# Image 0's values copied whole and split on GpSimd, with three other steps of the start moved

## Chip, cores and metric

The kernel runs on one core of a Trainium2 chip. The metric is the device time of one execution in microseconds, as the median of several. The profile is one more execution with the hardware profiler on. The engines are TensorE (PE; PEld is its weight load), VectorE (DVE), ScalarE (ACT), GpSimd (POOL) and SyncE (SP), which issues most transfers.

## What is computed

Two layers over x of shape 4 x 128 x 32 x 32 (four images, C = 128 channels, 1024 pixels), float32:

```python
# layer 0, without softmax: g, theta, phi are 1x1 convolutions to 64 channels
pairwise_weight = jnp.matmul(theta_x, phi_x) / N
y = jnp.matmul(pairwise_weight, g_x)
out = x_flat + _conv1x1(y, out_w, out_b)
# layer 1, on layer 0's output x (g = x)
scores = jnp.einsum('ncp,ncq->npq', theta, phi) / jnp.sqrt(c)
attn = jax.nn.softmax(scores, axis=-1)
f = jnp.einsum('npq,ncq->ncp', attn, g)
return x + conv1x1(f, conv1_w, conv1_b)
```

## The kernel before

Layer 0 has no softmax, so for each image it folds into one affine map of x: Z = (I + A) x + d, where A comes from the inner product of phi and g over all pixels. Per image the chain is pg0, pg1 (phi and g of the two halves of x), MT (their inner product), R, A, then Z0, Z1 (two halves of 512 pixels). Layer 1 takes Z: t = U Z + u are the queries with theta and phi folded together, V holds the values with the last convolution folded in, and rho is a row term (one more column of the value product) which goes into the exponent's shift.

Each image has 8 tiles of 128 query rows, 32 tiles in all, numbered n. For a tile: scores(n) (six matmuls of 512 columns into the PSUM `ring`, slot n % 2); row_max(n) on DVE; row_shift(n) on POOL, 128 x 1, from the row maximum and rho; exps(n) on ACT, which also sums the rows; norm(n) on DVE, a reciprocal and a multiplication of P in place; turn(n), eight transposes into the PSUM `turned`; high_turned and low_turned (ACT, DVE), which split the result; and attend, which after every four tiles multiplies values with the turned probabilities into the PSUM bank `numer`. Scores of n + 2 are issued ahead of the turning of n.

Products of float32 precision are made from rounded parts (type fp32r): a value X is split into X_hi, a rounded copy, and X_lo = X - X_hi, and `three` multiplies hi by hi, lo by hi and hi by lo. The rounding is a copy (ACT, or POOL as CAST), the low part a subtraction (DVE or POOL). POOL works on SBUF only here.

All small products of an image pass one after the other through one PSUM bank, `aux`, in the order of `AUX_ORDER`: each is issued on PE when its predecessor has left the bank (`aux_free`). Every engine's program is one list written out by hand, in which `early_job(b, t)` and `late_job(b, t)` place image b's steps in the tiles of image b - 1. An instruction waits for those ahead of it on its engine.

Around the change: image 0's values come in three parts of 3, 3 and 2 chunks of 128 pixels (`V_PARTS`). Parts 0 and 1 go through `numer`, which is free until the first attend, part 2 through `aux` at tile 1. For each, DVE makes the row term (L649), ACT makes V_hi (L506) and DVE V_lo (L654). On PE the start is: phi and g of image 1, t part 0 (one tile), scores(0), value part 0 (L281), t part 1 (three tiles, `turned`), aux job t1 (the rest of t), scores(1), then the loop over n. POOL joins Z from its parts for image 0 (L799), rounds x of image 1 (`high_x` L818, `low_x` L822) in tiles 0 and 1, and splits Z of image 1 (`split_z`, L828 and L830) in tiles 3 and 4. Other lines: L234 inner product, L222 to L224 the three matmuls of `three`, L317 turn, L336 attend, L521 exps, L529 and L682 split of the turned tile, L557 and L712 t of image 0, L643 t_lo, L638 AT_lo, L667 row maximum, L673 and L675 norm, L811 shift. SP's `load(3)` (L193 on) waits for both low parts of image 1's x, whose buffer it overwrites.

## Time and profile before

| | us |
|---|---|
| median of 3 runs | 175.65 (175.43 to 176.45) |
| the profiled execution | 174.63 |
| its span, first to last instruction | 172.8 |
| PE busy in it | 161.3 |
| granted TensorE clock | 1.00 throughout |

The profile's page gives busy time by engine, a strip of 40 slices (4.32 us each) and the costliest groups of instructions. The trace behind it is read by views: busy time by stage, who waited for whom, the timeline. In a timeline row the first number is the start, the second the duration; brackets hold the idle time of the engine just before and what ended it. Durations of queued instructions overlap a little, so distances between starts are the safer measure of pace.

### The profile page before, as it was taken

Reading aid. Unit: us, or ns where it says so; the run is one execution under the profiler, and the core shown is the slowest. Engines: PE = TensorE matmul, PEld = TensorE weight load, DVE = VectorE, ACT = ScalarE, POOL = GpSimd, SP = SyncE. Lnnn points to the kernel's source line nnn. Section 1 sums busy time; section 2 is a strip of 40 time slices with the busy share of each in tenths; the row PEclk is TensorE's granted clock in tenths of the full one; section 3 lists DMA queues with packets and bytes.
Section 4 is the critical chain, followed back from the end, with each engine's and each line's share of the span. In section 5 each row is a group of like instructions: output and inputs, shape, how many; then the busy total and the mean of one; then the engine's idle time right before and its main releaser. Section 6 shows DMA issues by size and latency. Waiting matters only on the chain.

```text
span 172.8 us, 2602 instructions
## 1 busy us (share of the span) xinstructions
PE 161.3 (93%) x967; PEld 134.2 (78%) x967; DVE 126.2 (73%) x217; ACT 95.1 (55%) x178; POOL 64.9 (38%) x73
## 2 busy tenths in 40 slices
PE   7789893986999999999999999999999999998994
PEld 6667682765888898787888898787898888886893
DVE  1316698779698897567898887567899889899512
ACT  3024554576765572567766573567766566667410
POOL 1006016526622257226624256216625252834020
PEclk9999999999999999999999999999999999999999
DMA  4703000020000001000000101000000101000111
GB/s 138 197 0 121 4 0 0 14 109 0 4 2 0 0 4 61 0 0 0 4 0 0 61 4 63 0 0 0 4 0 4 61 0 65 0 0 0 61 61 64
DMA packets 2829, 4.76 MB, mean 28 GB/s; under 512 B 448, under 2 KB 1280, under 8 KB 2816
## 3 DMA queue, kind: packets, MB, share of 16 engines
q1 hardware_dynamic: 2304, 4.39, 7.2%
q10 hardware_dynamic: 512, 0.20, 0.7%
q8 instruction: 8, 0.13, 0.3%
q14 instruction: 5, 0.04, 0.1%
HBM read 2.49 MB, written 2.10 MB: 27 GB/s over the span
## 4 chain that ended last, share of the span: by engine, by line
PE 83%; DVE 8%; DMA 3%; POOL 2%; ACT 2%; issue 1%; SPq 0%; ACTq 0%
PE numer L336 22%; PE turned L317 15%; PE ring L222 8%; PE ring L224 8%; PE ring L223 8%; DVE negmax L667 3%; PE aux L281 3%; DMA X<-x_dram 3%; PE aux L228 3%; PE aux L343 2%; PE aux L234 2%; PE aux L222 2%; PE aux L223 1%; PE aux L224 1%; DVE P L675 1%; PE ring L383 1%
## 5 line engine op out<-in xcount | busy, mean ns | idle before, releaser
L811 POOL TENSOR_SCALAR shift<-negmax,rho 128x1 f32<-128x1 f32 x32 | 27.9, 871 | 82.7 <-DVE negmax L667 78.1
L667 DVE TENSOR_REDUCE negmax<-ring 128x1 f32<-128x1024 f32 x32 | 39.1, 1223 | 18.5 <-PE ring L224 18.1
L521 ACT ACTIVATE P<-ring,shift 128x1024 f32<-128x1024 f32 x32 | 35.8, 1119 | 9.8 <-POOL shift L811 9.6
L682 DVE TENSOR_TENSOR PT_lo<-turned,PT_hi 128x512 fp32r<-128x512 f32 x62 | 39.8, 681 | 0.9 <-ACT PT_hi L529 0.9
L529 ACT ACTIVATE PT_hi<-turned 128x512 fp32r<-128x512 f32 x62 | 33.7, 596 | 9.3 <-PE turned L317 9.3
L317 PE MATMUL turned<-identity,P 128*128 128x128 f32 x256 | 33.6, 274 | 0.6 <-DVE PT_lo L682 0.6
L317 PEld LDWEIGHTS turned<-identity,P 128*128 128x128 f32 x256 | 29.5, 141 | 4.0 <-DVE P L675 1.0
L222 PE MATMUL ring<-Z_hi,t_hi 128*128 128x512 f32 x64 | 26.5, 414 | 0.6 <-DVE t_lo L712 0.6
L224 PE MATMUL ring<-Z_lo,t_hi 128*128 128x512 f32 x64 | 25.2, 394 | 0.0
L223 PE MATMUL ring<-Z_hi,t_lo 128*128 128x512 f32 x64 | 25.1, 393 | 0.0
L675 DVE TENSOR_SCALAR P<-P,rden 128x1024 f32<-128x1024 f32 x32 | 24.1, 754 | 1.1
L336 PE MATMUL numer<-PT_hi,V_hi 128*128 128x512 f32 x56 | 24.4, 435 | 0.0
L336 PE MATMUL numer<-PT_lo,V_hi 128*128 128x512 f32 x56 | 22.1, 395 | 0.0
L336 PE MATMUL numer<-PT_hi,V_lo 128*128 128x512 f32 x56 | 22.1, 394 | 0.0
L222 PEld LDWEIGHTS ring<-Z_hi,t_hi 128*128 128x128 f32 x64 | 12.0, 188 | 3.9 <-DVE t_lo L712 1.2
L224 PEld LDWEIGHTS ring<-Z_lo,t_hi 128*128 128x128 f32 x64 | 12.0, 188 | 2.8
L223 PEld LDWEIGHTS ring<-Z_hi,t_lo 128*128 128x128 f32 x64 | 12.1, 188 | 2.2
L336 PEld LDWEIGHTS numer<-PT_hi,V_lo 128*128 128x128 f32 x56 | 10.5, 187 | 2.5
L336 PEld LDWEIGHTS numer<-PT_lo,V_hi 128*128 128x128 f32 x56 | 10.6, 190 | 1.3
L336 PEld LDWEIGHTS numer<-PT_hi,V_hi 128*128 128x128 f32 x56 | 10.6, 189 | 1.3
L838 POOL TENSOR_TENSOR result<-attended,Z 128x512 f32<-128x512 f32 x7 | 9.0, 1287 | 4.2 <-ACT attended L539 4.2
L501 ACT ACTIVATE t_hi<-aux,U 128x512 fp32r<-128x512 f32 x7 | 4.8, 689 | 9.1 <-PE aux L224 9.1
(116 smaller groups left out, 198.0 us busy)
## 6 DMA issues: line engine op xcount, KB each, us to landing
out_dram<-result SPq DMA_DIRECT2D x7, 256.0 KB, 2.0
X<-x_dram SPq DMA_DIRECT2D x3, 512.0 KB, 3.3
X<-x_dram SPq DMA_DIRECT2D x2, 256.0 KB, 4.4
out_dram<-result SPq DMA_DIRECT2D x1, 192.0 KB, 1.9
w<-weights_dram SPq DMA_DIRECT2D x1, 128.0 KB, 5.8
wi<-inner_dram ACTq DMA_DIRECT2D x1, 64.2 KB, 5.6
pg_w<-pg_weights_dram ACTq DMA_DIRECT2D x1, 64.0 KB, 3.6
pg_b<-pg_bias_dram ACTq DMA_DIRECT2D x1, 64.0 KB, 5.6
```

The costliest lines, as they stand in the source:

```text
L222: nc.tensor.matmul(to, left_hi, right_hi[:, cols], start=first, stop=False)
L223: nc.tensor.matmul(to, left_lo, right_hi[:, cols], start=False, stop=False)
L224: return nc.tensor.matmul(to, left_hi, right_lo[:, cols], start=False, stop=last)
L317: mm = nc.tensor.transpose(turned[:, j * TILE:(j + 1) * TILE], P[:, n % P_BUFFERS, j * TILE:(j + 1) * TILE], identity[:, :])
L336: mm = nc.tensor.matmul(numer[:, :], left[:, b % 2, chunk], right[:, g, j, :], start=(j == 0 and n == 0), stop=(j == TILES - 1 and n == 2))
L521: nc.scalar.activation(P[:, n % P_BUFFERS, :], ring[:, n % 2, :], ACT.Exp, bias=shift[:, t:t + 1], accum_out=den[:, t:t + 1]).then_inc(pro ...
L529: nc.scalar.activation(PT_hi[:, group % GROUPS, half_chunks(half), k * TILE:(k + 1) * TILE], turned[:, columns(half)].rearrange("p (j r) - ...
L667: nc.vector.tensor_reduce(negmax[:, t:t + 1], ring[:, n % 2, :], AX.X, ALU.max, negate=True).then_inc(max_ready, 1)
L675: nc.vector.tensor_scalar(P[:, n % P_BUFFERS, :], P[:, n % P_BUFFERS, :], rden[:, t:t + 1], None, ALU.mult).then_inc(probs_normed, 1)
L682: nc.vector.tensor_tensor(PT_lo[:, group % GROUPS, half_chunks(half), rows], turned[:, columns(half)].rearrange("p (j r) -> p j r", j=CHUN ...
L811: nc.gpsimd.tensor_scalar(shift[:, t:t + 1], negmax[:, t:t + 1], rho[:, b % 2, t:t + 1], rho[:, b % 2, t:t + 1], ALU.subtract, ALU.add).th ...
L838: nc.gpsimd.tensor_tensor(result[:, g, :], attended[:, g, :], Z[:, b % Z_BUFFERS, columns(g)], ALU.add).then_inc(result_ready, 1)
```

## The change

Image 0's value part 2 leaves `aux` for `numer`, as the other two. ACT now makes the row term of each part and one plain copy of the part into V_plain (the buffer that was V_last), in place of V_hi; the copy frees `numer`. POOL makes V_hi and V_lo of image 0 from V_plain, part by part, behind row_shift(0), (2) and (4). DVE makes neither for image 0. On PE, t part 1 is issued ahead of value part 0, the aux job t1 behind scores(1), value part 1 still behind turn(0) and value part 2 behind turn(1); on DVE t1's low part comes behind row_max(2). On POOL x of image 1 is rounded ahead of the joins of Z and its low parts are made before and after row_shift(0); Z of image 1 is split in tiles 2 and 3. attend(0, 0) waits for three low parts of V. The other images are treated as before.

```diff
@@ -52,10 +52,10 @@
 JOBS = ("pg0", "pg1", "MT", "R", "A", "Z0", "Z1", "t0", "V0", "V1", "V2", "t1")
-AUX_ORDER = ([(0, "MT"), (0, "R"), (0, "A"), (1, "pg0"), (0, "t1"), (0, "V2")] + [(1, job) for job in JOBS[2:]]
+AUX_ORDER = ([(0, "MT"), (0, "R"), (0, "A"), (1, "pg0"), (0, "t1")] + [(1, job) for job in JOBS[2:]]
              + [(b, job) for b in range(2, IMAGES) for job in JOBS])
 
-SPLIT_ORDER = [(b, job) for b, job in AUX_ORDER if job in ("t0", "V0", "V1", "V2", "t1") or (job == "A" and b)]
+SPLIT_ORDER = [(b, job) for b, job in AUX_ORDER if job in ("t0", "t1") or (b and job in ("A", "V0", "V1", "V2"))]
 
@@ -114,7 +114,7 @@
         PT_lo = sb("PT_lo", [C, GROUPS, TILES, BANK], F32R)
-        V_last = sb("V_last", [C, PIX])
+        V_plain = sb("V_plain", [C, PIX])
         PT_last = sb("PT_last", [C, TILES, TILE])
@@ -144,7 +144,8 @@
         first_t, first_t_hi, first_t_lo = sem("first_t"), sem("first_t_hi"), sem("first_t_lo")
-        first_v, first_v_hi, first_v_lo = sem("first_v"), sem("first_v_hi"), sem("first_v_lo")
+        first_v, first_v_copied = sem("first_v"), sem("first_v_copied")
+        first_v_hi, first_v_lo = sem("first_v_hi"), sem("first_v_lo")
         first_rho = sem("first_rho")
@@ -323,8 +324,9 @@
                         if b == 0:
-                            pe.wait_ge(first_v_lo, 2)
-                        pe.wait_ge(aux_free, aux_after(b, "V2"))
+                            pe.wait_ge(first_v_lo, len(V_PARTS))
+                        else:
+                            pe.wait_ge(aux_free, aux_after(b, "V2"))
                     if group >= 1:
@@ -389,19 +391,19 @@
             scores(0)
+            queries(0, first_t_bank(1), FIRST_T[1]).then_inc(first_t, 1)
             pe.wait_ge(first_z_ready, 1)
...
             value_chunks(0, numer, 0).then_inc(first_v, 1)
-            queries(0, first_t_bank(1), FIRST_T[1]).then_inc(first_t, 1)
+            scores(1)
             job_t(0, 1)
-            scores(1)
-
-            def first_value_part():
-                pe.wait_ge(first_z_ready, 2)
-                pe.wait_ge(first_v_lo, 1)
-                value_chunks(0, numer, 1).then_inc(first_v, 1)
+
+            def first_value_part(part):
+                pe.wait_ge(first_z_ready, HALVES)
+                pe.wait_ge(first_v_copied, part)
+                value_chunks(0, numer, part).then_inc(first_v, 1)
 
@@ -420,8 +422,8 @@
             def late_job(b, t):
-                if t == 0 and b == 1:
-                    job_V(0, 2)
+                if t == 1 and b == 1:
+                    first_value_part(2)
                 if t == 0 and b > 1:
@@ -442,7 +444,7 @@
                 if n == 0:
-                    first_value_part()
+                    first_value_part(1)
                 if n >= GT:
@@ -462,7 +464,7 @@
                 for j in half_range(half):
-                    mm = nc.tensor.matmul(last_tile, V_last[:, j * C:(j + 1) * C], PT_last[:, j, :],
+                    mm = nc.tensor.matmul(last_tile, V_plain[:, j * C:(j + 1) * C], PT_last[:, j, :],
                                           start=(j == 0), stop=(j == TILES - 1))
@@ -557,15 +559,26 @@
 
-            def first_v_high(part):
-                act.wait_ge(first_rho, part + 1)
-                high_values(0, numer, part, first_v_hi)
+            def first_row_terms(part):
+                act.wait_ge(first_v, part + 1)
+                first, last = V_PARTS[part]
+                nc.scalar.activation(rho[:, 0, first:last].rearrange("p (j c) -> p j c", c=1),
+                                     chunks_of(numer, part)[:, :, C:C + 1], ACT.Identity,
+                                     bias=r0).then_inc(first_rho, 1)
+
+            def first_values(part):
+                if part:
+                    first_row_terms(part)
+                first, last = V_PARTS[part]
+                nc.scalar.activation(V_plain[:, first * C:last * C].rearrange("p (j c) -> p j c", c=C),
+                                     chunks_of(numer, part)[:, :, 0:C], ACT.Copy).then_inc(first_v_copied, 1)
 
...
             first_t_high(1)
+            first_row_terms(0)
             exps(0)
-            first_v_high(0)
+            first_values(0)
             high_t(0, 1)
@@ -584,10 +597,10 @@
             def late_job(b, t):
-                if t == 0 and b == 1:
-                    high_V(0, 2)
                 if t == 1:
                     copy_R(b)
+                if t == 1 and b == 1:
+                    first_values(2)
                 if t == 2:
@@ -606,7 +619,7 @@
                 if n == 0:
-                    first_v_high(1)
+                    first_values(1)
                 if n + 2 < ALL:
@@ -713,14 +726,6 @@
 
-            def first_v_low(part):
-                dve.wait_ge(first_v_hi, part + 1)
-                low_values(0, numer, part, first_v_lo)
-
-            def first_row_terms(part):
-                dve.wait_ge(first_v, part + 1)
-                row_terms(0, numer, part).then_inc(first_rho, 1)
-
             first_z_low(0)
@@ -729,13 +734,9 @@
             row_max(0)
-            dve.wait_ge(u_copied, 1)
-            first_row_terms(0)
             first_t_low(1)
...
             row_max(1)
-            first_v_low(0)
-            low_t(0, 1)
 
@@ -750,8 +751,6 @@
             def late_job(b, t):
-                if t == 0 and b == 1:
-                    low_V(0, 2)
                 if t == 0 and b > 1:
@@ -765,15 +764,13 @@
                     row_max(n + 2)
+                if n == 0:
+                    low_t(0, 1)
                 norm(n + 1)
...
                 low_turned(n, 0)
-                if n == 0:
-                    first_row_terms(1)
                 low_turned(n, 1)
-                if n == 0:
-                    first_v_low(1)
             dve.wait_ge(turned_ready, ALL * HALVES)
@@ -784,6 +781,17 @@
         def _(pool):
+            def high_x(b):
+                pool.wait_ge(x_loaded[b], 16)
+                if b >= 2:
+                    pool.wait_ge(aux_free, aux_after(b - 1, "Z1"))
+                nc.gpsimd.tensor_copy(X_hi[:, :], X[:, b % 2, :]).then_inc(x_hi, 1)
+
+            def low_x(b, half):
+                pool.wait_ge(x_hi, b)
+                nc.gpsimd.tensor_tensor(X_lo[:, columns(half)], X[:, b % 2, columns(half)],
+                                        X_hi[:, columns(half)].bitcast(F32), ALU.subtract).then_inc(x_lo, 1)
+
             nc.gpsimd.memset(identity[:, :], 0.0).then_inc(identity_ready, 1)
@@ -794,33 +802,24 @@
             nc.gpsimd.tensor_tensor(UT_lo[:, :], U[:, 0:C], UT_hi[:, :].bitcast(F32), ALU.subtract).then_inc(u_lo, 1)
+            high_x(1)
             for half in range(HALVES):
...
                                         Z_lo[:, 0, columns(half)].bitcast(F32), ALU.add).then_inc(first_z_ready, 1)
+            low_x(1, 0)
 
...
                 if t in (0, 3, 6):
-                    if b == 0 and t < 6:
+                    if b == 0:
                         pool.wait_ge(first_rho, t // 3 + 1)
...
                                         rho[:, b % 2, t:t + 1], ALU.subtract, ALU.add).then_inc(shift_ready, 1)
-
-            def high_x(b):
-                pool.wait_ge(x_loaded[b], 16)
-                if b >= 2:
-                    pool.wait_ge(aux_free, aux_after(b - 1, "Z1"))
-                nc.gpsimd.tensor_copy(X_hi[:, :], X[:, b % 2, :]).then_inc(x_hi, 1)
-
-            def low_x(b, half):
-                pool.wait_ge(x_hi, b)
-                nc.gpsimd.tensor_tensor(X_lo[:, columns(half)], X[:, b % 2, columns(half)],
-                                        X_hi[:, columns(half)].bitcast(F32), ALU.subtract).then_inc(x_lo, 1)
 
@@ -838,7 +837,18 @@
 
+            def split_first_values(part):
+                first, last = V_PARTS[part]
+                cols = slice(first * C, last * C)
+                pool.wait_ge(first_v_copied, part + 1)
+                nc.gpsimd.tensor_copy(V_hi[:, 0, cols], V_plain[:, cols]).then_inc(first_v_hi, 1)
+                pool.wait_ge(first_v_hi, part + 1)
+                nc.gpsimd.tensor_tensor(V_lo[:, 0, cols], V_plain[:, cols], V_hi[:, 0, cols].bitcast(F32),
+                                        ALU.subtract).then_inc(first_v_lo, 1)
+
             row_shift(0)
+            low_x(1, 1)
+            split_first_values(0)
             row_shift(1)
@@ -847,18 +857,20 @@
                 if i + 1 < IMAGES:
-                    if t == 0:
+                    if t == 0 and i:
                         high_x(i + 1)
                         low_x(i + 1, 0)
-                    if t == 1:
+                    if t == 1 and i:
                         low_x(i + 1, 1)
-                    if t == 3:
+                    if n in (0, 2):
+                        split_first_values(1 if n == 0 else 2)
+                    if t == (3 if i else 2):
                         split_z(i + 1, 0)
-                    if t == 4:
+                    if t == (4 if i else 3):
                         split_z(i + 1, 1)
...
                     pool.wait_ge(aux_free, aux_after(i, "t1"))
-                    nc.gpsimd.tensor_tensor(V_last[:, :], V_hi[:, i % 2, :].bitcast(F32),
+                    nc.gpsimd.tensor_tensor(V_plain[:, :], V_hi[:, i % 2, :].bitcast(F32),
                                             V_lo[:, i % 2, :].bitcast(F32), ALU.add).then_inc(v_joined, 1)
```

## Rows read from the trace of the kernel before

**Rows 1.** The page: span, busy time by engine, PE's tenths in 40 slices.

```profile
span 172.8 us, 2602 instructions
...
PE 161.3 (93%) x967; PEld 134.2 (78%) x967; DVE 126.2 (73%) x217; ACT 95.1 (55%) x178; POOL 64.9 (38%) x73
...
PE   7789893986999999999999999999999999998994
```

**Rows 2.** Busy time by stage: length, busy us of PE, PEld, DVE, ACT, POOL.

```profile
60.00:80.00 20.00, 20.00 (x127) 16.81 (x126) 15.10 (x26) 12.01 (x23) 9.06 (x10) 1.00 0.04 14
```

**Rows 3.** Who waited for whom, 14 to 50 us: total us, times, longest.

```profile
PE aux L234 <- DVE V_lo L654: 2.9, 1, 2.9
...
PE aux L222 <- POOL Z_lo L830: 1.4, 1, 1.4
...
PE aux L222 <- DVE AT_lo L638: 0.7, 1, 0.7
```

**Rows 4.** Timeline, first values and t: start, duration, instruction [idle before].

```profile
17.72 0.83 PE L281 MATMUL numer<-VW,Z 128*128 128x130 f32 x6
...
18.31 0.42 PE L222 MATMUL turned<-Z_hi,UT_hi 128*128 128x384 f32 x1
...
19.12 0.58 ACT L557 ACTIVATE t_hi<-turned,U 128x384 fp32r<-128x384 f32 x1 [3.32 <-PE turned L224]
19.38 0.37 POOL L811 TENSOR_SCALAR shift<-negmax,rho 128x1 f32<-128x1 f32 x1 [2.12 <-DVE rho L649]
...
19.73 0.62 DVE L712 SCALAR_TENSOR_TENSOR t_lo<-turned,U,t_hi 128x384 fp32r<-128x384 f32 x1 [0.46 <-ACT t_hi L557]
...
20.41 0.50 PE L222 MATMUL ring<-Z_hi,t_hi 128*128 128x512 f32 x1 [0.64 <-DVE t_lo L712]
```

**Rows 5.** Timeline, 27 to 30 us, ACT, DVE and PE around the long wait.

```profile
27.20 0.49 ACT L506 ACTIVATE V_hi<-numer 128x384 fp32r<-128x384 f32 x1 [1.19 <-DVE rho L649]
27.58 1.11 ACT L521 ACTIVATE P<-ring,shift 128x1024 f32<-128x1024 f32 x1
...
29.23 0.41 DVE L654 TENSOR_TENSOR V_lo<-aux,V_hi 128x256 fp32r<-128x256 f32 x1
...
29.70 1.15 PE L234 MATMUL aux<-pgT 128*64 128x64 f32 x16 [2.89 <-DVE V_lo L654]
```

**Rows 6.** Timeline, 21 to 31 us: norm(0), turn(0), scores(3), a shift.

```profile
21.23 0.75 DVE L675 TENSOR_SCALAR P<-P,rden 128x1024 f32<-128x1024 f32 x1
...
23.27 1.04 PE L317 MATMUL turned<-identity,P 128*128 128x128 f32 x8
...
25.18 0.48 PE L222 MATMUL ring<-Z_hi,t_hi 128*128 128x512 f32 x1
...
30.95 0.92 POOL L811 TENSOR_SCALAR shift<-negmax,rho 128x1 f32<-128x1 f32 x1 [2.02 <-DVE negmax L667]
```

**Rows 7.** Timeline, then groups by shape (busy us, mean ns | idle before).

```profile
27.66 1.27 POOL L822 TENSOR_TENSOR X_lo<-X,X_hi 128x512 fp32r<-128x512 f32 x1
27.72 0.56 DVE L654 TENSOR_TENSOR V_lo<-numer,V_hi 128x384 fp32r<-128x384 f32 x1
...
L799 POOL TENSOR_TENSOR Z<-Z_hi,Z_lo 128x512 f32<-128x512 f32 x2 | 2.5, 1282 | 1.3 <-DVE Z_lo L705 1.3
...
L828 POOL CAST Z_hi<-Z 128x512 fp32r<-128x512 f32 x2 | 1.2, 609 | 0.0
```

**Rows 8.** Timeline, 30 to 46 us: turn(1), row maxima, image 1's t, values.

```profile
30.77 1.09 PE L317 MATMUL turned<-identity,P 128*128 128x128 f32 x8
...
33.85 1.23 DVE L667 TENSOR_REDUCE negmax<-ring 128x1 f32<-128x1024 f32 x1 [0.47 <-PE ring L224]
...
41.83 1.21 DVE L667 TENSOR_REDUCE negmax<-ring 128x1 f32<-128x1024 f32 x1
...
42.93 0.47 PE L222 MATMUL aux<-Z_hi,UT_hi 128*128 128x512 f32 x1 [1.37 <-POOL Z_lo L830]
...
45.97 0.83 PE L281 MATMUL aux<-VW,Z 128*128 128x130 f32 x6
```

## Prediction

> **What bounds the kernel now.** I read four views, from coarse to fine. The page first: TensorE (PE) is busy for 93% of a span of 172.8 us, no other engine comes near [rows 1]. So only time in which PE stands still can be won, unless PE work goes away, and this change takes none away: it has the same matmuls in another order. Its PE line in 40 slices of 4.32 us falls to 3 tenths at 25.9 to 30.2 us and to 6 tenths at 38.9 to 43.2, and is at 9 from there to the tail [rows 1]. Then the busy time by stage: from 60 to 80 us PE is busy for 20.00 of 20.00 us [rows 2]. The room lies in the start, before 46 us, and in the tail, which the diff leaves alone. Third, who waited for whom from 14 to 50 us: PE stood for 2.9 us before the inner product of image 1 (L234) until DVE's V_lo, 1.4 us before t of image 1 until POOL's Z_lo and 0.7 us before Z of image 1 until DVE's AT_lo [rows 3]. The fourth is 0.64 us before scores(1) until t_lo [rows 4]. Together 5.6 us, the most that any reordering of the start could give. Last, the timeline around each wait, for what the releaser itself waited for.
>
> The 2.9 us wait is a long queue. Image 0's values come in three parts. Part 2 sits in the aux bank, which the inner product needs next. Its V_hi on ACT is queued behind exps(2) at 27.58, which is queued behind V_hi of part 1 at 27.20. That one waited 1.19 us for a row term on DVE; V_lo of part 2 ends at 29.64 and PE starts at 29.70 [rows 5].
>
> **The change, part by part.** Times below are of the profiled execution.
>
> *Start.* PE now does the second part of t ahead of value part 0. Value part 0 took from 17.72 to 18.31, when t started; so t starts 0.6 earlier, t_hi ends at 19.1 instead of 19.70, and t_lo follows the row maximum on DVE, at about 19.1 instead of 19.73 [rows 4]. scores(1), before at 20.41, starts at 19.8. But the aux job t1, half of scores(1)'s work, used to lie in the wait ahead of scores(1) and now comes behind it. scores(1) and (2) took 2.86 us together (20.41 to 23.27), so t1 is 0.7, and 19.8 + 2.86 + 0.7 puts turn(0) at 23.35, against 23.27 before [rows 4, 6]. So the start gives nothing to PE; the move costs 0.1.
>
> *The first row term on ACT.* Value part 0 now ends at about 19.15, and ACT makes the term (0.2 us) once t_hi is through. No row has an ACT operation on so few PSUM columns; the bounds are nothing and the 0.49 of V_hi's 384 columns [rows 5]; I take 0.2, nearer the low end, since three columns leave little but the fixed part. Shift(0) then starts at 19.5 instead of 19.38 [rows 4]: exps(0) and norm(0) 0.1 late.
>
> *V_hi, V_lo and row terms leave DVE, a copy takes V_hi's place on ACT.* The ACT copy has V_hi's shape and costs the same 0.49 [rows 5]: nothing. DVE loses three subtractions (0.56, 0.56 and 0.41 us) and three row terms [rows 5, 7]. It is not the bound there, and row_max(2), which stood behind two low parts, starts at 23.6, as soon as scores(2) is ready.
>
> *The split on POOL.* No row has it at 384 columns. The cast took 609 ns for 512 and the subtraction 1.27 us for 512 [rows 7]. Scaled by columns they are 0.46 and 0.96, unscaled 0.61 and 1.27; I take 0.5 and 1.0, near the scaled ends. Part 0's split stands ahead of shift(1) on POOL, and behind it wait exps(1), norm(1) and scores(3). The copy ends at 21.5 on ACT; at that time norm(0) is running on DVE, from 21.3 to 22.1. A shift that meets a norm takes 0.92 where one alone takes 0.37, ending about 0.15 after the norm [rows 4, 6]. So I let the cast begin when the norm is over: 22.1 to 22.6, V_lo to 23.65, shift(1) 23.7 to 24.1 (row_max(1) is done at 23.25). Then exps(1), 1.1 plus the 0.1 until its sums are read, to 25.3, and scores(3) at 25.4 instead of 25.18, PE waiting some 0.4 us for it. With an unhindered cast shift(1) could start at 23.25, which gives 0.3 to 0.4 back; with both unscaled prices it is 0.4 later.
>
> The Trainium skill (SBUF — State Buffer, section "SBUF: two separate sides") says that a DVE operation in a two-port mode and a GpSimd operation hold the shared port pair exclusively, whichever starts first, for the whole instruction. On its first half the trace agrees (0.92 beside a norm, 0.37 alone); that a norm waits behind a POOL operation no row here shows. The same notes (GPSIMD Engine Reference, "Engine selection") advise VectorE for elementwise work, GpSimd being about 2 times slower with two inputs, which speaks against this change; the trace agrees in size, 1.27 us for 512 columns on POOL beside 0.56 for 384 on DVE [rows 7]. By it each subtraction costs some 0.4 us more than on DVE; only part 0's is on the path, and it is in the 0.4 above.
>
> *The wait of 2.9 us.* Part 2 leaves the aux bank, so the inner product waits only for t1's low part. That is placed behind row_max(2): 24.75 to 25.5, before PE gets there. scores(3) from 25.4, the inner product from 26.9 and, with the 1.07 it took from 29.70 to 30.77, turn(1) at 27.95: 2.8 early [rows 5, 8]. Is turn(1) ready? norm(1) ends at 26.4; the low parts of turn(0) end at 27.0 and 27.6. Yes, with 0.3 to spare, and this slack is what covers DVE. Value part 2 now stands behind turn(1): 0.36 us, work that was ahead of scores(3) before. So scores(4) starts 2.5 early, and row_max(4) at 31.35 instead of 33.85 [rows 8]. On POOL, part 1 is split from 27.0 to 28.6 and shift(3) is wanted at 28.9: hidden, by 0.3.
>
> *Rounding of x earlier.* high_x(1) fills POOL's idle 1.3 us before the joins of Z (two half casts of 609 are 1.2) [rows 7]; low_x fills 17.3 to 18.5 and 19.9 to 21.2. Nobody waits. SyncE's load(3), queued behind load(2), waits for both low parts and is released some 12 us earlier; its next store is far off and the queues are empty then. Nothing.
>
> *Z's split one step earlier.* POOL: shift(4) to 33.6 beside norm(3), part 2's split (256 columns, about 1.15) to 34.8, then Z half 0, which ACT makes at 35.5 (before, 2.5 later). Cast and subtraction, 0.6 and 1.3, end at 37.5. PE reaches t of image 1 at 38.9. So the wait of 1.4 us at 42.93 goes, and t starts 4.0 early [rows 3, 8]. The AT_lo wait of 0.7 stays: its chain (scores(4), row maximum, norm, AT_lo) is only shifted. Shift(5) is now behind this split; row_max(5) ends at 37.35, so it is at most 0.1 to 0.2 late, with norm(4) beside it.
>
> *What is late next.* Value part 0 of image 1 needs aux free from t's low part, which DVE makes after row_max(6) and norm(5). Row_max(6) was at 41.83 and moves by 2.5 only, to 39.3, norm(5) ends at 41.4, t_lo at 42.1. PE is there at 41.7: 0.4 of waiting. Value part 0 starts at 42.2 instead of 45.97 [rows 8], and behind it all goes as before, PE full until the tail.
>
> **The sum.** 2.9 + 1.4 less 0.1 (start), 0.1 (scores(3), net of the value part moved behind it) and 0.4 (new wait) is 3.7. The profiled execution had 174.63 us around its 172.8 us span; less 3.7 it is 170.9. The median of three runs is 1.0 higher, 175.65, and from it I predict 171.9.
>
> **Rivals.** (a) *The lock tie, 172.3.* Z_lo of half 0 ends at 37.5, norm(4) wants to start at 37.45. If a norm waits behind a POOL operation and the queued shift slips in first, norm(4) is 0.4 late, and with it row_max(6) and value part 0: gain 3.3. By the skill's rule it would be so; the times are too near to tell. (b) *Unhindered cast, 171.5*: gain 4.1, as above. (c) *Slow splits, 172.7*: unscaled prices in part 0, and part 1's split then in front of shift(3); 0.4 each, gain 2.9. (d) *Half, 173.2*: the 1.4 us is replaced by another wait of the same size (Z half 0 late on ACT behind exps(4), or shift(5) behind the split): gain 2.4. For it: exps(4) and the split are tight in the chain; against it: 1.4 us of room at 38.9. (e) *Nothing, 175.6*: the new ACT and POOL steps set the pace of all early tiles, each exps about 0.6 late over six tiles. Against it: POOL was idle most of this stretch. (f) *Slower, 177*: DVE and POOL exclude each other for all that POOL now does from 19.9 to 37.5, about 7.3 us (1.3 + 1.5 + 1.5 + 1.15 + 1.9), also where DVE runs subtractions, and each exclusion lands on the path. It turns to a loss once more than 3.7 of the 7.3 do; 5 would give 177. Against it: the DVE subtraction at 27.72 took 0.56 for 384 columns with POOL at work beside it (1.5 ns a column), the one at 29.23 took 0.41 for 256 with POOL idle (1.6 a column) [rows 5, 7].
>
> **How the numbers follow.** Forecast 0.44, (a) 0.16, (b) 0.10, (c) 0.11, (d) 0.11, (e) 0.05, (f) 0.03. The range from 171.0 to 173.4 takes in (b) and (d), with 0.5 at the low end for the spread of the runs. About 0.5%, 0.9 us, is what a measurement of this kernel can tell from no change: faster by more 0.92, within 0.05, slower 0.03.
>
> **What would show it.** Of the changed kernel the waits view should have no wait of PE L234 on V_lo, none of t on Z_lo, AT_lo's 0.7 still there, a new wait of about 0.4 before scores(3), released by exps(1), and one of about 0.4 before value part 0 of image 1, released by t_lo. turn(1) should start near 27.95, t of image 1 near 38.9, the value part near 42.2. The POOL cast of part 0 should be lengthened or delayed by norm(0), and the one of part 1 not. Wrong would be the prediction if POOL's split takes over 2 us a part, if the ACT row term costs over half a microsecond, or if PE has new gaps after 46 us.

## The result, and the profile after

| | before | after |
|---|---|---|
| median, us | 176.05 (175.43 to 176.75, 4 executions) | 170.51 (170.28 to 170.84, 4 executions) |
| the profiled execution | 174.63 | 170.84 |
| its span | 172.8 | 169.0 |

The ratio is 0.9686, with a 95% interval of 0.9639 to 0.9733. The forecast was 171.9, and the measured time lies below its range, which began at 171.0. The 176.05 is the median of the three executions known before and a fourth. The two traces differ by 3.8 us, where the sum gave 3.7; the medians differ by 5.5. So there are two questions: whether the 3.8 us went where the prediction said, and where the other 1.7 us come from.

The page of the changed kernel, span, engines and the PE and clock lines of the 40 slices (of 4.2 us each):

```profile
span 169.0 us, 2605 instructions
...
PE 161.8 (96%) x967; PEld 135.2 (80%) x967; DVE 124.1 (73%) x211; ACT 95.8 (57%) x181; POOL 69.1 (41%) x79
...
PE   7889899799999999999999999999999999998994
...
PEclk9999999999999999999999999999999999999999
```

The 3 and the 6 of [rows 1] are gone; PE's busy time is nearly what it was (161.8 and 161.3 us), and the span is 3.8 us shorter.

Who waited for whom from 14 to 50 us, rows of PE, of its weight load and POOL's for the copy on ACT (total us, times, longest):

```profile
POOL V_hi L844 <- ACT V_plain L573: 1.9, 2, 1.5
...
PE aux L223 <- DVE AT_lo L651: 0.9, 1, 0.9
...
PE ring L223 <- DVE t_lo L725: 0.7, 1, 0.7
...
PEld aux L282 <- DVE t_lo L656: 0.5, 1, 0.5
```

The 2.9 and the 1.4 of [rows 3] are not there. AT_lo's wait is still there, 0.9 where 0.7 was, and so is t_lo's before scores(1).

The timeline of the changed kernel, the steps that the prediction put a time to (start, duration):

```profile
19.70 0.50 PE L223 MATMUL ring<-Z_hi,t_hi 128*128 128x512 f32 x1 [0.66 <-DVE t_lo L725]
...
21.29 0.75 DVE L688 TENSOR_SCALAR P<-P,rden 128x1024 f32<-128x1024 f32 x1
...
21.50 0.90 POOL L844 CAST V_hi<-V_plain 128x384 fp32r<-128x384 f32 x1 [0.42 <-ACT V_plain L573]
...
22.48 1.01 POOL L846 TENSOR_TENSOR V_lo<-V_plain,V_hi 128x384 fp32r<-128x384 f32 x1
...
23.27 1.03 PE L318 MATMUL turned<-identity,P 128*128 128x128 f32 x8
...
23.49 0.36 POOL L821 TENSOR_SCALAR shift<-negmax,rho 128x1 f32<-128x1 f32 x1
...
25.23 0.47 PE L223 MATMUL ring<-Z_hi,t_hi 128*128 128x512 f32 x1 [0.25 <-ACT P L523]
...
26.66 0.50 POOL L844 CAST V_hi<-V_plain 128x384 fp32r<-128x384 f32 x1 [1.50 <-ACT V_plain L573]
...
26.79 1.15 PE L235 MATMUL aux<-pgT 128*64 128x64 f32 x16
...
27.86 1.09 PE L318 MATMUL turned<-identity,P 128*128 128x128 f32 x8
...
31.39 1.22 DVE L680 TENSOR_REDUCE negmax<-ring 128x1 f32<-128x1024 f32 x1 [0.80 <-PE ring L225]
...
33.79 0.50 PE L223 MATMUL aux<-X_hi,AT_hi 128*128 128x512 f32 x1 [0.95 <-DVE AT_lo L651]
```

and further on:

```profile
38.94 0.39 PE L223 MATMUL aux<-Z_hi,UT_hi 128*128 128x512 f32 x1
...
42.16 0.94 PE L282 MATMUL aux<-VW,Z 128*128 128x130 f32 x6
```

| step | before | predicted | measured |
|---|---|---|---|
| scores(1) | 20.41 | 19.8 | 19.70 |
| turn(0) | 23.27 | 23.35 | 23.27 |
| shift(1) | 23.43 | 23.7 | 23.49 |
| scores(3) | 25.18 | 25.4 | 25.23 |
| turn(1) | 30.77 | 27.95 | 27.86 |
| row_max(4) | 33.85 | 31.35 | 31.39 |
| t of image 1 | 42.93 | 38.9 | 38.94 |
| value part 0 of image 1 | 45.97 | 42.2 | 42.16 |

Every step is within about 0.2 us. The reader should see three things in the rows. The inner product (L235) starts at 26.79, behind scores(3) and nothing else. The cast of value part 0 took 0.90 us, because it began 0.2 us into norm(0), and the same cast at 26.66, with no norm beside it, took 0.50. And value part 0 of image 1 is held by t_lo, the new last comer: its weight load waits 0.5 us, PE itself loses less (t to value part took 3.04 us before and takes 3.22).

So the first question, where the 3.8 us went, is answered by the traces. The experiments are mostly about the second, and about which part of the change carries which part of the 3.8 us.

### The profile page after: what moved, and what is told of

It is laid out like the page before. It is cut to its first block, busy times and chain, and to the rows that moved or that the text cites. A ratio compares the mean times of both kernels' runs of the same rounds, so it can differ in the third digit from the quotient of the medians.

```text
span 169.0 us, 2605 instructions
## 1 busy us (share of the span) xinstructions
PE 161.8 (96%) x967; PEld 135.2 (80%) x967; DVE 124.1 (73%) x211; ACT 95.8 (57%) x181; POOL 69.1 (41%) x79
## 4 chain that ended last, share of the span: by engine, by line
PE 84%; DVE 7%; DMA 3%; ACT 2%; POOL 2%; issue 1%; SPq 0%; ACTq 0%
PE numer L338 22%; PE turned L318 14%; PE ring L223 9%; PE ring L225 8%; PE ring L224 8%; PE aux L282 4%; DMA X<-x_dram 3%; DVE negmax L680 3%; PE aux L229 3%; PE aux L345 2%; PE aux L235 2%; PE aux L223 2%; DVE P L688 2%; ACT P L523 1%; PE aux L225 1%; PE aux L224 1%
## 5 line engine op out<-in xcount | busy, mean ns | idle before, releaser
L695 DVE TENSOR_TENSOR PT_lo<-turned,PT_hi 128x512 fp32r<-128x512 f32 x62 | 39.7, 681 | 0.4 <-ACT PT_hi L531 0.4
```

Of the source, the lines that this page charges most:

```text
L695: nc.vector.tensor_tensor(PT_lo[:, group % GROUPS, half_chunks(half), rows], turned[:, columns(half)].rearrange("p (j r) -> p j r", j=CHUN ...
```

## The experiments

Each is timed beside the kernel before, on one chip for each group. Ratios are to the kernel before of that group.

### The kernel before once more

No edit. 

> The kernel before, unchanged, once more, for its spread. Theory A (its first profiled execution, 172.8 us, was a short one, and the others lose the difference somewhere): spans of 172.8 to 174.9 us, most of them over 173.5, and a trace in which some wait is longer than in the first. Theory B (the first trace is typical and the gap between 3.8 us by spans and 5.5 us by medians is chance of the chips): spans within 0.3 us of 172.8 and a ratio to itself of 1.000.

Measured: 175.66 us as itself (10 executions, 174.07 to 177.18), and 175.37 (173.88 to 176.90) in the 19 executions that stood beside the group; ratio 1.0037 (0.9990 to 1.0085). The times fall into clusters, and the mean granted clock of each execution tells which:

| granted clock of the execution | executions of the 29 | us |
|---|---|---|
| 1.00 | 10 | 173.88 to 174.21, one of 174.95 |
| 0.99 | 16 | 175.15 to 176.18 |
| 0.98 or, once, 0.99 | 3 | 176.58 to 177.18 |

The first profiled execution of the kernel before had clock 1.00 throughout. The one of this run did not. Its busy time by stage (length, busy us and instructions of PE, PEld, DVE, ACT, POOL, then the granted clock, DMA share and GB/s):

```profile
26.00:28.00 2.00, 0.06 (x1) 0.00 (x0) 1.51 (x4) 1.57 (x4) 1.91 (x2) 1.00 0.00 0
28.00:30.00 2.00, 1.07 (x12) 1.07 (x13) 1.67 (x4) 0.29 (x2) 0.16 (x1) 0.82 0.00 0
30.00:32.00 2.00, 2.00 (x14) 1.88 (x13) 0.83 (x3) 0.49 (x2) 1.81 (x2) 0.50 0.00 0
32.00:34.00 2.00, 2.00 (x10) 1.32 (x9) 1.38 (x2) 1.75 (x3) 0.34 (x1) 0.83 0.30 88
34.00:36.00 2.00, 2.00 (x17) 1.66 (x15) 1.34 (x3) 0.86 (x5) 0.05 (x1) 1.00 0.45 174
```

and its timeline on PE:

```profile
25.66 0.40 PE L224 MATMUL ring<-Z_lo,t_hi 128*128 128x512 f32 x1
28.93 1.72 PE L234 MATMUL aux<-pgT 128*64 128x64 f32 x16 [2.87 <-DVE V_lo L654]
30.58 1.97 PE L317 MATMUL turned<-identity,P 128*128 128x128 f32 x8
32.48 0.51 PE L250 MATMUL aux<-wi,MT 128*64 128x128 f32 x2
32.92 0.50 PE L222 MATMUL ring<-Z_hi,t_hi 128*128 128x512 f32 x1
```

PE stands from 26.06 to 28.93. The wait is as long as in the first trace (2.87 and 2.89 us). But behind it the granted clock is 0.50, that is 1.2 GHz where it was 2.4: the inner product takes 1.72 us instead of 1.15 and turn(1) 1.97 instead of 1.09. From the inner product's start to that of scores(4) it is 3.99 us, against 2.46 (29.70 to 32.16) in the first trace. The fall costs 1.5 us here, on top of the wait. Theory A holds for the spread, not for its reason: no wait is longer, the clock is lower. The median of the kernel before is that of an execution with the fall, and its first trace, on which the sum was made, is of one without.

The two traces differ in a second thing. In the first, PE waited at the start for the load of x, in this one hardly (its weight load 0.2 us), and image 1's first matmuls, which stand ahead of anything that the change moves on PE, started 0.76 us later in the first. From the waits of the first trace up to 14 us, then the first line of those matmuls in the first trace and in this one:

```profile
PE ring L228 <- DMA X<-x_dram: 1.0, 1, 1.0
```

```profile
13.79 1.05 PE L228 MATMUL aux<-pg_w,X 128*128 128x128 f32 x8
```

```profile
13.03 1.05 PE L228 MATMUL aux<-pg_w,X 128*128 128x128 f32 x8
```

So the first profiled execution, of 174.63 us, belongs to neither cluster: it had no fall, but a late start, and lies 0.6 us above the median of those at clock 1.00 (174.0). In all 13 traces these matmuls start between 12.95 and 13.85 us. Counted from there to the end of the span, so that the start drops out, the kernel before took 159.0 us in the first trace and 160.5 in this one. The same count is used below beside the medians.

### The changed kernel beside it

No edit. 

> The changed kernel, unchanged, on the same chip as the kernel before. If the gain is the 3.8 us that the two traces show: ratio 0.978 (171.9 for 175.7). If the kernel before loses 1 to 2 us more in most executions and the changed one doesn't: ratio 0.968 to 0.972.

Measured: 170.43 us (170.18 to 170.90), clock 1.00 in all four; ratio 0.9746 (0.9660 to 0.9833), between the two that were expected, since a good part of the executions beside it had no fall. Against those at clock 1.00 (173.9 to 174.2) the changed kernel is 3.6 us faster, against those at 0.99 about 5.4. Counted from image 1's first matmul its trace has 155.4 us, the first of the changed kernel 155.3.

### Z of image 1 split late

```diff
-                    if t == (3 if i else 2):
+                    if t == 3:
                         split_z(i + 1, 0)
-                    if t == (4 if i else 3):
+                    if t == 4:
                         split_z(i + 1, 1)
```

> The changed kernel with Z of image 1 split in tiles 3 and 4 again, behind row_shift(5) and (6). Theory (the early split ended the wait of t of image 1): shift(5) ends at 38.4, the split of half 0 at 40.3, t starts at 40.4 instead of 38.94, the wait of 1.4 us on Z_lo is back, and the kernel is 1.3 us slower than the changed one. Rival (the wait went because the values left DVE and ACT, not because of the split's place): no difference.

Measured: 172.15 us (171.74 to 173.48), clock 1.00; ratio 0.9863 (0.9779 to 0.9947). It is 1.7 us slower than the changed kernel of the same group, over the 1.3 expected; one of the four, at 173.48, pulls the median. Counted from image 1's first matmul its trace has 156.6 us against 155.3, and there the loss is the expected 1.3. The wait is back in the waits view:

```profile
PE aux L223 <- POOL Z_lo L829: 1.4, 1, 1.4
...
PE aux L223 <- DVE AT_lo L651: 0.9, 1, 0.9
```

The place of the split carries the 1.4 us, as the prediction had it.

### POOL's order alone

In the kernel before: `high_x(1)` ahead of the joins of Z, `low_x(1, 0)` behind them, `low_x(1, 1)` behind `row_shift(0)`, and `split_z` in tiles 2 and 3 for image 1 (as in the change's own diff). 

> The kernel before with only POOL's order changed: x of image 1 rounded ahead of the joins of Z, and Z of image 1 split in tiles 2 and 3. Theory: the wait of 2.9 us before the inner product stays, the wait of 1.4 us before t of image 1 goes, a new one of about 0.1 before value part 0 of image 1: 1.3 us faster than before, 0.993. Rival (the two waits hang together: without the first gain the second is nothing): no difference.

Measured: 174.31 us (173.10 to 176.01); ratio 0.9951 (0.9909 to 0.9993). In its trace the wait on V_lo is 2.9 us as before and the one on Z_lo is gone. Nine of its ten executions had a clock below 1.00, so medians compare badly; its one execution at 1.00 took 173.10, 0.9 us under those of the kernel before, and those at 0.99 took 173.99 to 174.84 against 175.15 to 176.18. Counted from image 1's first matmul, its trace (with the fall) has 159.1 us, that of e1_before (with the fall) 160.5. The gain is there, about 1.3 us, without the values' part.

### The wait filled

In the kernel before:

```diff
+                if t == 1 and b == 1:
+                    pe.wait_ge(turned_lo, HALVES)
+                    keep_warm(turned[:, 0:C], 16)
                 if t == 1:
                     job_MT(b)
```

> The kernel before with sixteen idle bfloat16 matmuls (no use is made of them) ahead of the inner product of image 1, started when the low parts of turn(0) are done, so that PE stands still for about 1 us instead of 2.9 and everything else, the late V_lo included, keeps its time. Clock theory (the wait of 2.9 us lets the granted clock fall to half in most executions, which costs about 1.7 us on top): clock 1.00 in nearly all executions, times 173.9 to 174.3, median some 1.5 us below the kernel before on the same chip. Rival (the spread comes from the transfers at the start and the fall is a bystander): the same spread of 173.9 to 176.9 and the same median.

Measured: 173.75 us (173.70 to 174.09), clock 1.00 in all four; ratio 0.9893 (0.9872 to 0.9915), 2.0 us under the 175.73 of its group, where 1.5 were expected. The first three of the same five stages:

```profile
26.00:28.00 2.00, 1.01 (x13) 0.60 (x12) 1.86 (x5) 1.22 (x2) 1.91 (x3) 1.00 0.00 0
28.00:30.00 2.00, 1.19 (x21) 1.02 (x19) 1.33 (x3) 0.64 (x3) 0.52 (x1) 1.00 0.00 0
30.00:32.00 2.00, 2.00 (x19) 1.59 (x17) 1.50 (x4) 1.17 (x3) 1.47 (x2) 1.00 0.00 0
```

```profile
27.40 1.07 PE L349 MATMUL turned<-idle 128*128 128x128 bf16 x16 [0.99 <-DVE PT_lo L685]
29.28 1.15 PE L234 MATMUL aux<-pgT 128*64 128x64 f32 x16 [0.81 <-DVE V_lo L657]
```

V_lo is as late as ever, and the inner product starts no earlier: 3.27 us behind the last matmul of scores(3), as in the first trace (3.28). Only PE no longer stands in one piece: 0.99 us, then sixteen useless matmuls, then 0.81 us. The clock stays at 2.4 GHz, the spread, 2.6 us in this group and 3.3 over all, shrinks to 0.4 and the median falls by 2 us. Counted from image 1's first matmul it takes 158.9 us, the time of the first trace without a fall (159.0). That settles the second question: what was missing in the sum is the fall of the clock behind the wait.

### The values alone

In the changed kernel: x rounded in tiles 0 and 1 and Z split in tiles 3 and 4, as before. 

> The changed kernel with x of image 1 rounded in tiles 0 and 1 and Z split in tiles 3 and 4, as before: only the values and the order on PE are changed. Clock 1.00 throughout, time that of the late Z split alone (172.1). POOL's cast of x (1.03 us) now starts at about 25.2, just before norm(1) at 25.46. Lock theory (a norm waits for a POOL operation that began first): norm(1) starts or ends at about 26.2 to 26.9, turn(1) 0.3 us later than 27.9, total +0.2 to +0.4. Rival (only POOL gives way): norm(1) at 25.46 for 0.75, and +0.

Measured: 171.58 us (171.28 to 172.05), clock 1.00; ratio 0.9768 (0.9741 to 0.9795). The values' way and PE's order carry all of the gain but the 1.4 us of Z's split; the earlier rounding of x is worth nothing that can be seen (counted from image 1's first matmul, 156.7 us here and 156.6 with Z split late alone). It did show how a norm and POOL exclude each other. DVE and POOL of this kernel from 24 to 28 us:

```profile
24.68 1.23 DVE L688 TENSOR_SCALAR P<-P,rden 128x1024 f32<-128x1024 f32 x1
```

```profile
24.32 1.04 POOL L788 CAST X_hi<-X 128x1024 fp32r<-128x1024 f32 x1
25.45 1.60 POOL L792 TENSOR_TENSOR X_lo<-X,X_hi 128x512 fp32r<-128x512 f32 x1
```

The cast began first and ran its usual 1.04 us. norm(1), where a norm takes 0.75 in the median of the 32, is recorded with 1.23, ending 0.55 us behind the cast; the subtraction behind that took 1.60 instead of 1.28. So the waiting goes both ways. The 0.2 to 0.4 us that it was expected to cost did not come: turn(1) follows the inner product by 1.08 us, against 1.07 in the changed kernel, since it had slack.

### The gap put into the changed kernel

```diff
                 if t == 1:
+                    if b == 1:
+                        pe.wait_ge(probs_normed, 3)
                     job_MT(b)
```

> The changed kernel in which PE waits for norm(2) before the inner product of image 1, which nothing needs: a gap from 26.7 to about 29.45, like that of the kernel before, with all else changed as it is. Clock theory: some 2.65 us slower in executions at clock 1.00 (173.0) and about 4.3 slower (174.7) in those where the clock falls, which should be a third to two thirds of them. Rival (the fall belongs to something else in the kernel before, its loads or its DVE queue): 2.65 slower in all, clock 1.00.

Measured: 174.98 us (174.51 to 176.18); ratio 0.9981 (0.9941 to 1.0020). The clock was below 1.00 in all eight executions, more often than expected. Its stages:

```profile
28.00:30.00 2.00, 0.45 (x7) 0.46 (x8) 1.46 (x3) 0.00 (x0) 1.29 (x2) 1.00 0.00 0
30.00:32.00 2.00, 2.00 (x20) 1.93 (x19) 0.00 (x0) 0.65 (x2) 0.00 (x0) 0.72 0.00 0
32.00:34.00 2.00, 2.00 (x9) 1.44 (x8) 1.38 (x2) 1.74 (x4) 0.00 (x0) 0.50 0.00 0
```

```profile
29.55 1.15 PE L235 MATMUL aux<-pgT 128*64 128x64 f32 x16 [2.56 <-DVE P L690]
30.62 1.76 PE L318 MATMUL turned<-identity,P 128*128 128x128 f32 x8
```

A wait of 2.56 us, for something that nothing needs, brings back both losses: the kernel is 4.5 us slower than the changed one and as slow as the one before, with every other part of the change in place. Counted from image 1's first matmul the loss is 4.3 us, as expected for an execution with the fall: the inner product starts 2.6 us later, the rest comes behind it.

### The low parts ahead of the norm

In the changed kernel, on DVE:

```diff
+                if n in (2, 4):
+                    early_job(b + 1, t)
                 norm(n + 1)
-                if n and b + 1 < IMAGES:
+                if n and n not in (2, 4) and b + 1 < IMAGES:
                     early_job(b + 1, t)
```

> The changed kernel with AT_lo (tile 2) and t_lo of image 1 (tile 4) ahead of the norm on DVE, to end the two waits of PE that are left at Z (0.95 us) and at value part 0 (0.5 us). Theory (DVE's order sets both): Z of image 1 starts at 33.0 instead of 33.79, value part 0 at 40.9 instead of 42.16, 1.2 us faster than the changed kernel. Rival (the later norms turn into the next wait): less than 0.5 us.

Measured: 169.66 us (169.27 to 169.91), clock 1.00; ratio 0.9656 (0.9627 to 0.9686); once more in the last group:

> The kernel with AT_lo and t_lo first once more, beside the others of this group: 169.7, 0.8 us or so under the changed kernel's 170.5.

Measured: 169.52 us (169.39 to 169.73); ratio 0.9636 (0.9597 to 0.9675). PE's waits for AT_lo and before value part 0 are gone; these two of PE's are left in the waits view:

```profile
PE ring L223 <- DVE t_lo L725: 0.7, 1, 0.7
...
PE ring L223 <- ACT P L523: 0.3, 1, 0.3
```

It is about 0.9 us faster than the changed kernel, somewhat less than the 1.2 expected. Z starts 0.9 us earlier. But the weight load of Z's second half now waits 0.4 us for ACT's copy of the first, which costs PE 0.25, and the hold before value part 0 gives back about 0.3, not the 0.5 of its weight load.

### Value part 2 in the aux bank again

In the changed kernel, part 2 is multiplied into `aux` behind part 1, ACT takes it from there behind exps(2), and the inner product waits for that copy:

```diff
                 if t == 1:
+                    if b == 1:
+                        pe.wait_ge(first_v_copied, 3)
                     job_MT(b)
...
-                if t == 1 and b == 1:
+                if t == 0 and b == 1:
                     first_value_part(2)
```

> The changed kernel with value part 2 of image 0 in the aux bank again, issued behind part 1 as before, so that the inner product waits for ACT's copy of it (the split stays on POOL). Queue theory (what the inner product waited for was ACT's place behind exps(2), and leaving aux is what ends it): the copy comes behind exps(2), which ends at 27.7, with its row term to about 28.3; the inner product starts at 28.4 instead of 26.8, and the kernel is 1.2 to 1.6 us slower than the changed one (171.6 to 172.0), at clock 1.00. Rival (the fast split alone ends the wait): within 0.3 us of the changed kernel.

Measured: 171.35 us (171.16 to 171.36), clock 1.00; ratio 0.9736 (0.9698 to 0.9775). That is 0.8 to 0.9 us over the changed kernel. From its waits and its timeline:

```profile
PE aux L235 <- ACT V_plain L578: 0.6, 1, 0.6
```

```profile
24.71 0.68 PE L282 MATMUL aux<-VW,Z 128*128 128x130 f32 x4 [0.52 <-DVE t_lo L661]
...
26.93 0.43 ACT L578 ACTIVATE V_plain<-aux 128x256 f32<-128x256 f32 x1
27.41 1.01 PEld L235 LDWEIGHTS aux<-pgT 128*64 128x64 f32 x16 [1.05 <-ACT V_plain L578]
27.41 1.15 PE L235 MATMUL aux<-pgT 128*64 128x64 f32 x16 [0.63 <-ACT V_plain L578]
```

(Image 1's first matmul starts 0.75 us earlier in this trace than in that of the changed kernel.) The copy stands behind exps(2), and the inner product waits 0.63 us for it. But part 2 also has to wait for the aux bank itself, 0.52 us until DVE's t_lo has left it, and that makes scores(3) 0.7 us later. Counted from image 1's first matmul, the inner product starts 1.4 us later than in the changed kernel, 0.45 of which comes back because no value part stands behind turn(1), and the whole takes 1.0 us more. So the direction is that of the queue theory, and its wait behind exps(2) is about half of the delay; the theory had no wait for t_lo. Leaving the aux bank is worth 0.9 us, both waits taken together; that the rest of the 2.9 went with the steps taken off DVE, the row terms and the subtraction, is read from the traces and was not tried by itself.

### POOL's shift ahead of the split

The kernel with the low parts first, and besides:

```diff
-            scores(1)
             job_t(0, 1)
+            scores(1)
...
-            split_first_values(0)
             row_shift(1)
+            split_first_values(0)
```

> The kernel with AT_lo and t_lo first, and besides it aux job t1 ahead of scores(1) again and POOL's row_shift(1) ahead of the split of value part 0. Theory (scores(3) waits for exps(1), which waits for the shift, and the order of t1 on PE is worth nothing by itself): shift(1) 0.25 us earlier, scores(3) at about 24.95 against 25.2, 0.25 us faster than with AT_lo and t_lo first alone. Rival A (t1 in the gap is won whole): 0.7 us faster. Rival B (the split now delays row_shift(2) and exps(2)): the same or slower.

Measured: 169.36 us (169.28 to 169.44), clock 1.00; ratio 0.9625 (0.9579 to 0.9671), 0.16 us under the kernel with the low parts first in the same group, the fastest of all, though the two overlap (169.39 to 169.73 and 169.28 to 169.44). Counted from image 1's first matmul, scores(3) starts 0.2 us earlier, where 0.25 was expected, and the whole takes 154.2 us against 154.3. The 0.66 us before scores(1) are gone from its waits and stand before scores(3) instead:

```profile
PE ring L223 <- ACT P L523: 0.7, 1, 0.7
```

So what PE's order wins before scores(1), PE loses again before scores(3), because exps(1) releases scores(3) in either order. That the order is worth nothing by itself, as the prediction had it, is read from these waits; both edits were made at once, and neither was timed alone.

## Why the prediction was wrong

**The mechanism was right, and the sum of 3.7 came out, in part by luck.** The long wait went, the wait on Z_lo went, a hold by t_lo came, and scores(3) was released by exps(1), all as predicted. The sum of 3.7 stands against 3.8 by the traces and 3.6 by executions at clock 1.00. Its terms, beside what the distances between the starts of matmuls give:

| term of the sum | us in the sum | us by starts |
|---|---|---|
| the wait before the inner product (from scores(3) on) | +2.9 | +2.96 |
| the wait on Z_lo (from Z to t of image 1) | +1.4 | +1.52 |
| the start, up to turn(0) | -0.1 | -0.06 |
| scores(3), less the value part that left its front | -0.1 | -0.05 |
| the same value part behind turn(1) | not in it | -0.45 |
| the hold by t_lo (from t to the scores behind value part 0) | -0.4 | -0.29 |

The fifth term is missing in the sum. It credits the 0.36 us that value part 2 frees ahead of scores(3) and never charges them behind turn(1), though the prediction's own times do (turn(1) 2.8 early, scores(4) 2.5 early); with it the list gives 3.3. The other terms, each taken a little too low in gain or too high in loss, made up for it.

The profiled execution was forecast at 170.9 and took 170.84. That is luck in the last tenths too: both profiled executions started equally late (image 1's first matmul at 13.79 and 13.73), while this differs by up to 0.9 us from one trace to the next. Counted from there they differ by 3.7 us. Of the rivals, the lock tie (a) did not come: Z_lo ended at 37.54 and norm(4) started at 37.51 with its usual 0.75. Its mechanism exists (the values alone show it), only the tie fell the other way. The cast was held by norm(0) for 0.4 us, so (b) fell as well. The prices of the split were 0.50 (part 1's cast, which nothing held) and 1.01, as taken.

**The step that failed is the last one.** The prediction says: "The median of three runs is 1.0 higher, 175.65, and from it I predict 171.9." That carries the 1.0 us over to the changed kernel as a constant. It was no constant. It was the cost of a fall of the granted clock to 1.2 GHz behind the 2.9 us wait, which most executions have and the profiled one had not (1.5 us by the traces, 1.7 by the medians of the two clusters), less some 0.6 us by which the profiled one lies above the others without a fall, most likely its late start. The clocks of the first executions (175.43 to 176.75) are not on record; their times are those of executions with the fall. The change takes away the wait, and so the fall. Of the 1.4 us between forecast and median, 1.0 is this step, and 0.3 is that the profiled execution of the changed kernel is the slowest of its four. The runs show the fall from four sides:

| kernel | longest wait of PE, us | executions | with clock below 1.00 |
|---|---|---|---|
| before, in the groups above | 2.9 | 46 | 33 |
| before with POOL's order alone | 2.85 | 10 | 9 |
| changed, with the gap | 2.6 | 8 | 8 |
| before, the wait filled | 1.4 (the one on Z_lo) | 4 | 0 |
| changed, Z split late, and values alone | 1.4 | 8 | 0, within 0.002 |
| changed and its other variants | 1.0 | 24 | 0, within 0.001 |

(One execution of the kernel before, of 320 us at clock 1.00, is left out; nothing on record explains it.) Nothing in the single trace that the prediction had showed a clock below 1.00. But two numbers beside it did not fit: the profiled execution was 0.8 us below the lowest of three others, and those three spread over 1.0 us in a kernel that is one fixed order of work. A rival "the other executions lose a further 1 to 2 us at the wait, and the change ends that as well" would have given 175.65 less 3.7 less 1.0, 170.9 and below, and the range should have reached it. The forecast should also have been built from the profiled execution's own 174.63, which was the only number that the sum belonged to.

Smaller misses. AT_lo's wait grew from 0.65 to 0.95 us where it was to stay at 0.7, at no cost: from scores(4) to Z it is 4.10 us before and 4.09 after, as the prediction said of the chain; before, PE had lost the missing 0.3 us ahead of that, at the R step. PE came to value part 0 of image 1 at 41.9, not 41.7, so that the hold was shorter than taken. ACT's row term took 0.26 us, where 0.2 was taken.

## What to carry to other kernels

Compare the profiled execution with the others before the sum: if it lies outside their spread, find what they have that it has not, for that part does not follow the sum. Count from a point that the change can't move, so that the spread of the start drops out. And check a sum against the step times that it was made from: each must have every term of the other. A wait of the matmul engine of 2.6 to 2.9 us, in a stage that is otherwise full, cost its length plus 1.5 to 2 us in most executions of these kernels; between 1.4 and 2.5 us nothing was tried. It was cured even where the late result could not be brought forward, with useless matmuls in the middle of it. When an operation is moved into a shared bank's queue, look at what is queued ahead of the one who empties the bank.

## What the runs showed of the hardware

- The same wait of 2.87 to 2.89 us was followed by 2.4 GHz in one traced execution and by 1.2 GHz in the next. Over 46 executions the clock fell in 33. In 36 executions of kernels with no wait over 1.4 us the mean granted clock was never under 0.998; behind an artificial wait of 2.56 us it fell in 8 of 8. Why the shorter wait did it more often than the longer one is not settled: in that kernel other work surrounds it.
- A few executions of the kernel before took 176.5 to 177.2 us with a mean clock of 0.98 (once 0.99). Whether the fall is longer there or there is a second one was not traced.
- The start of the program differs from execution to execution: image 1's first matmul starts at 12.95 to 13.85 us in the 13 traces. In the first trace PE waited 1.0 us for x. In that of e2_after it waited for no load that long, but the sixteen matmuls of phi and g of image 0 took 3.47 us, where they took 2.93 in that of e1_before. What sets their pace was not tested.
- DVE's multiplication from SBUF to SBUF and POOL's operations exclude each other whichever starts first: 1.23 us instead of 0.75 for a norm begun behind a cast, 0.90 instead of 0.50 for a cast begun behind a norm. This is the second half of the rule that the prediction cites from the Trainium skill (SBUF — State Buffer, "SBUF: two separate sides"), and the trace now agrees with it. DVE's subtractions with one operand in PSUM were not held: the two of a turned tile (L695) took 1.28 us together at 26.13 in the changed kernel, with POOL's cast and subtraction beside them, and 1.28 at 29.31 with POOL at work only for their first 0.3 us.
